# Even products ahead of the match-replaces, and the lag correlation through a stationary inverse matrix, a ScalarE copy and TensorE transposes

## What is computed

```
corr = ifft(fft(q) * conj(fft(k))).real        # q = layernorm(x), k = v = ctx, along the 64 positions
w, idx = top_k(corr, 8); w = softmax(w)        # per sequence and channel, 8 of 64 lags
out = sum_i w[i] * v[min(idx[i] + pos, 63)]    # the context shifted by each chosen lag
x = x + out
x = x + moe(layernorm(x))                      # 2 of 16 experts a token, and a shared expert
```

## Time and profile before

| | us |
|---|---|
| median of 3 runs | 483.29 (482.85 to 485.19) |
| profiled execution | 485.63 |
| its span | 483.7 |

### The profile page before, as it was taken

The page is one execution under the profiler, slowest core; times in us unless marked ns, Lnnn a source line. Parts: engine busy times, 40 slices in busy tenths (PEclk is TensorE's granted clock), DMA queues, the critical chain, the costliest instruction groups (busy, mean ns, idle before and its releaser), DMA issues.

```text
span 483.7 us, 9087 instructions
## 1 busy us (share of the span) xinstructions
PE 434.3 (90%) x2640; PEld 335.3 (69%) x2640; DVE 303.2 (63%) x960; ACT 217.5 (45%) x456; POOL 256.4 (53%) x311
## 2 busy tenths in 40 slices
PE   4698888888888887899999989999999899999992
PEld 2445555555555555478888969998889899878891
DVE  3768888888888877468676234443343443426975
ACT  4545666556666563263022114464454565722120
POOL 2556666666666663002787500778857561044772
PEclk9889999999999999999999998999999999999997
DMA  8411244444444432061776654788888885255896
GB/s 325 175 45 65 68 152 154 152 168 171 173 171 172 169 126 74 22 252 76 246 274 231 226 197 117 251 268 291 303 286 294 244 272 177 100 158 169 271 300 211
DMA packets 39295, 91.83 MB, mean 190 GB/s; under 512 B 4432, under 2 KB 4432, under 8 KB 39120
## 3 DMA queue, kind: packets, MB, share of 16 engines
q1 hardware_dynamic: 32256, 64.25, 37.7%
q0 software_dynamic: 6992, 27.01, 17.8%
HBM read 49.82 MB, written 41.42 MB: 189 GB/s over the span
## 4 chain that ended last, share of the span: by engine, by line
PE 58%; DVE 18%; DMA 10%; issue 5%; POOL 4%; ACT 3%; DVEq 0%; POOLq 0%; SPq 0%; ACTq 0%
PE bank L408 33%; DMA y_rows<-sh_act 7%; PE bank L427 7%; PE bank L444 6%; DVE arena L887 5%; DVE top_v L877 4%; PE bank L572 3%; PE bank L417 3%; PE bank L419 3%; DMA arena<-y_rows,pos_i 2%; DVE arena L883 2%; POOL arena L1235 2%; PE bank L493 2%; DVE arena L893 2%; DVE arena L892 2%
## 5 line engine op out<-in xcount | busy, mean ns | idle before, releaser
L408 PE MATMUL bank<-tokens_hi,shw_hi 128*128 128x512 f32 (+1 forms) x160 | 56.3, 352 | 0.0
L408 PE MATMUL bank<-tokens_hi,shw_lo 128*128 128x512 f32 (+1 forms) x160 | 55.6, 347 | 0.0
L408 PE MATMUL bank<-tokens_lo,shw_hi 128*128 128x512 f32 (+1 forms) x160 | 55.6, 347 | 0.0
L1235 POOL DMA_INDIRECT arena<-y_rows,pos_i x32 | 32.4, 1013 | 42.2 <-DMA y_rows<-sh_act 27.2
L408 PE MATMUL bank<-w_hi,tokens_hi 128*128 x188 | 53.9, 287 | 0.6 <-issue 0.5
L408 PE MATMUL bank<-w_hi,tokens_lo 128*128 x188 | 53.7, 285 | 0.0
L408 PE MATMUL bank<-w_lo,tokens_hi 128*128 x188 | 53.6, 285 | 0.0
L1212 POOL DMA_INDIRECT xs_rows<-x2T,pos_i x32 | 37.0, 1156 | 28.8 <-DVE pos_i L1003 19.3
L1051 DVE TENSOR_TENSOR act_sb<-bank,silu_sb 128x128 f32<-128x128 f32 x47 | 13.7, 292 | 56.7 <-ACT silu_sb L759 51.5
L1198 POOL TENSOR_TENSOR w_lo<-x2T,w_hi 128x1536 fp32r<-128x1536 f32 x13 | 45.5, 3499 | 1.1
L1038 DVE TENSOR_TENSOR tokens_lo<-bank,tokens_hi 128x512 fp32r<-128x512 f32 x47 | 32.5, 692 | 19.8 <-ACT tokens_hi L753 19.6
(11 more groups left out here) (138 smaller groups left out, 1101.7 us busy)
## 6 DMA issues: line engine op xcount, KB each, us to landing
y_rows<-sh_act SPq DMA_DIRECT2D x47, 256.0 KB, 4.0
xs_rows<-act_lo SPq DMA_DIRECT2D x10, 1024.0 KB, 4.8
x2T<-w_exp POOLq DMA_DIRECT2D x13, 768.0 KB, 5.8
xg_sb<-xs_rows SPq DMA_DIRECT2D x24, 256.0 KB, 3.3
const_sb<-xs_rows SPq DMA_DIRECT2D x23, 256.0 KB, 4.6
resid<-x SPq DMA_DIRECT2D x16, 256.0 KB, 2.7
arena<-ctx SPq DMA_DIRECT2D x16, 256.0 KB, 3.3
x_rows<-arena SPq DMA_DIRECT2D x16, 256.0 KB, 2.1
```

Of the source, the lines that this page charges most:

```text
L408: last = mm(ps, a[i], b[k], start=start and n == 0, stop=stop and n == len(terms) - 1)
L1235: nc.gpsimd.indirect_dma_start(y_in[buf], None, y_rows[:, :], bass.IndirectOffsetOnAxis(ap=pos_i[:, col:col + 1], axis=0)).then_inc(y_gath ...
```

## The change

In the correlation, `C["corr"]` becomes the stationary matrix and the 512 channels stream, in two products (one for each sequence) into the halves of `ps_T`. The result has lags in the partitions. ScalarE copies it to `corr_prod[0]` at the head of its iteration, and four TensorE transposes turn it into `ps_corr`, in the form it had. Two semaphores are added, and a wait for the last reader of `ps_T`. On VectorE the match-replaces of pair `n` go behind the even products of pair `n − 1`.

```diff
--- before.py
+++ after.py
@@ -264,6 +264,7 @@
         w_even_psum, w_odd_psum = sem("w_even_psum"), sem("w_odd_psum")
         out_products_ready, out_psum, resid_ready = sem("out_products_ready"), sem("out_psum"), sem("resid_ready")
         x2n_ready, x2T_psum, x2T_ready = sem("x2n_ready"), sem("x2T_psum"), sem("x2T_ready")
+        lags_psum, lags_ready = sem("lags_psum"), sem("lags_ready")
         logits_psum, logits_ready = sem("logits_psum"), sem("logits_ready")
         route_step, route_diff, route_exp = sem("route_step"), sem("route_diff"), sem("route_exp")
         chosen_ready, counts_psum = sem("chosen_ready"), sem("counts_psum")
@@ -439,10 +440,14 @@
                     p, _ = pair(h, b, 0)
                     pe.wait_ge(products_ready, p + 1)
                     wait(pe, lags_marked, p)
+                    wait(pe, x2T_ready, p - 2)
+                    for s in range(2):
+                        last = mm(ps_T[s * L:(s + 1) * L, :], C["corr"], corr_prod[s], start=True, stop=True)
+                    last.then_inc(lags_psum, 1)
+                    pe.wait_ge(lags_ready, p + 1)
                     for c in range(KB):
-                        for s in range(2):
-                            last = mm(ps_corr[:, c * P + s * L:c * P + (s + 1) * L], corr_prod[s][:, c * P:(c + 1) * P], C["corr"],
-                                      start=True, stop=True)
+                        cols = slice(c * P, (c + 1) * P)
+                        last = nc.tensor.transpose(ps_corr[:, cols], corr_prod[0][:, cols], C["identity"])
                     last.then_inc(corr_psum, 1)
                 if n == PAIRS:
                     shared_half(0, 0, 0, range(2, KB))
@@ -678,6 +683,10 @@
                     normalise(0, xn, tile_of(resid, p), p, xn_ready)
 
             def iteration(h, b, n):
+                if live(n, 0):
+                    p, _ = pair(h, b, 0)
+                    act.wait_ge(lags_psum, p + 1)
+                    copy(corr_prod[0], ps_T[:, :]).then_inc(lags_ready, 1)
                 if live(n, -1):
                     p, _ = pair(h, b, -1)
                     act.wait_ge(lagwT_psum, p + 1)
@@ -881,16 +890,19 @@
                     largest = tops[:, :, 0:1]
                     tt(segs(top_e[:, :]), tops, largest.to_broadcast([P, SEGS, TOPK]), ALU.subtract)
                     tt(segs(expz), lags, largest.to_broadcast([P, SEGS, L]), ALU.subtract).then_inc(centered, 1)
-                    wait(dve, lagwT_psum, p)
-                    apart(dve, dve_passed)
-                    for s in range(SEGS):
-                        last = nc.vector.match_replace(segs(lagw)[:, s], tops[:, s], lags[:, s], TAKEN)
-                    last.then_inc(lags_marked, 1)
                 if live(n, -1):
                     p, pb = pair(h, b, -1)
                     dve.wait_ge(w_even_psum, p + 1)
                     tt(out_prod[0], ps_w_even[0][:, :], ctx_even[pb][0], ALU.mult)
                     tt(out_prod[1], ps_w_even[1][:, :], ctx_even[pb][1], ALU.mult).then_inc(out_products_ready, 1)
+                if live(n, 0):
+                    p, _ = pair(h, b, 0)
+                    wait(dve, lagwT_psum, p)
+                    apart(dve, dve_passed)
+                    lags, tops = segs(ps_corr[:, :]), segs(top_v[:, :])
+                    for s in range(SEGS):
+                        last = nc.vector.match_replace(segs(lagw)[:, s], tops[:, s], lags[:, s], TAKEN)
+                    last.then_inc(lags_marked, 1)
                 if n == 0:
                     products(h, b, n)
                 if live(n, 0):
```

## The result

| | before | after |
|---|---|---|
| median (runs) | 484.24 us (4) | 508.1 us (4; 507.31 to 508.76) |
| ratio after to before | | 1.049, 95% interval 1.0447 to 1.0534 |
| profiled execution, its span | 485.63, 483.7 | 507.31, 505.5 |
| granted clock over the span | 0.984 | 0.946 |
| TensorE busy (share) | 434.3 (90%) | 443.1 (88%) |

The change costs 23.9 us. The forecast was 497.3 with a range of 491 to 503: the direction was right, and the time lies above the range. Of the 10.8 us between them, 1.0 is the median of before, 484.24 here and 483.29 in the forecast.

The account below looks back on a forecast made before the run. The prediction took the longest circle of dependences in a loop turn to bound the kernel. Start +5.7, twelve turns +9.6 and end −1.3 made +14.0 us on 483.3, so 497.3 us, range 491 to 503.

Parts of the forecast that it names:

- The circle through ScalarE: Maxima, VectorE's list, GpSimd's root, normalisation, copy, transposes, maxima: 12.31 us a turn against 11.51, +9.6 us over 12 turns.
- The signs named for it: Copy 0.72 us behind normalisation, TensorE idle near 1.8 before transposes, VectorE some 1.5 before maxima, turn 12.3 us.
- rival C: Clock falls in the loop: about 1.9 us a turn, 520 us if every turn, 503 if three; chance 0.06.
- Rival B: Copy partly held, no wait before L892, start at full clock: 11.9 us a turn, 490.9 us; chance 0.10.
- The new wait before the even products: On VectorE, L892 waits 0.28 us for the even lag spectrum, which the match-replaces hid; bounds 0 and 0.45.
- The later marks: VectorE's marks come later by two even products; costed at nothing, up to 1.2 us without cover.
- Rival A: Copy not held, TensorE's circle decides: about 11.2 us a turn, 480.7 us in all; chance 0.08.
- The start: Up to the maxima of pair 2, at 40.6 instead of 34.86: +5.7 us, lower clock expected.
- The lower bound of 4.2 us: Least cost forecast up to the maxima of pair 2, reckoned with TensorE at full clock: +4.2 us.
- The end: Turn of pair 14: VectorE's 1.70 us wait before L917 shrinks, giving back 1.3 us (0.5 to 1.5).

Follow-up runs that it names:

- The order alone: Kernel before with only the match-replaces moved behind the even products, old correlation kept: 483.63 us beside 489.92, ratio 0.986.
- the correlation alone: Changed kernel with the match-replaces put back ahead of the even products, so only the new correlation: 500.73 us beside 489.92, ratio 1.0194.
- the filled kernel: Changed kernel plus eight TensorE products of constants between the correlation products and the wait for the copy: 504.59 us beside 489.92, ratio 1.0268.
- the second execution: Changed kernel run once more with nothing altered, beside the kernel before: 508.65 us beside 485.52, ratio 1.0486.
- the kernel with the copy first: Changed kernel with ScalarE's new copy moved ahead of the normalisation of x from pair 1 on: 486.09 us beside 489.92, ratio 0.9928.

## Why the prediction was right and wrong

*The circle through ScalarE: right.* Forecast 12.31 us a turn, measured 12.27 wherever the clock was full. The links held one by one: moments to normalisation 90.05 − 88.46 = 1.59 (forecast 1.58), normalisation to copy 0.72 (0.72), copy to transposes 91.38 − 90.77 = 0.61 (0.69), transposes to maxima 0.81 (0.77). The signs named for it are there in the turns at the full clock, with two differences of size: TensorE's idle time before the transposes was 2.0 and not 1.8, since the products came earlier than reckoned, and VectorE's before the maxima was 1.76 and not 1.5. The sign of rival C was there too: the clock from pair 2 to pair 14 was 0.89. Rival B, a circle only partly held with 11.9 us a turn, falls with the 12.27.

*The new wait before the even products: right.* Forecast 0.28 us; in the changed kernel L896 waits for the spectrum,

```profile
82.11 0.69 DVE L896 TENSOR_TENSOR arena<-bank,arena 128x512 f32<-128x512 f32 x1 [0.18 <-PE bank L428]
```

with 0.18 us idle and the rest of the 0.28 in handing over.

*The two halves apart: right.* The order alone gave 10.86 us a turn (10.7 in the expectation), the correlation alone 11.99 (12.0). The later marks, which the sum costs at nothing, were not tested apart.

*Rival A: rightly rejected; its price came out by luck.* With the copy unheld the kernel stood at 0.993 of before; the rival had said 480.7 us, which is 0.993 of 484.24. But its terms were off both ways: the twelve turns gave 131.35 − 138.07 = −6.7 us where it had −3.6, and the turn of pair 14 took 14.26 us instead of 12.78, +1.5 where it had −1.3.

*The start: right in size.* Maxima of pair 2 at 39.90 (40.6 forecast), with the lower clock as expected there. The lower bound of 4.2 us was ill worked out: by the rows that the forecast uses, the full clock takes off 1.1 us before the even spectrum and 0.94 before L892, which leaves 3.7.

*The end: wrong.* Forecast −1.3 us, measured +0.6. The clock explains part of it; but with the clock at 1.00 the turn still took 12.55 us, −0.2, in the filled kernel and in the second execution of the changed one. In the filled kernel the two subtractions (L931, L917 of before) started early, as forecast, and were slower:

```profile
197.57 2.51 DVE L931 TENSOR_TENSOR tokens_lo<-x2T,tokens_hi 128x512 fp32r<-128x512 f32 x2 [0.52 <-ACT tokens_hi L739]
197.93 1.60 POOL L1161 TENSOR_TENSOR tokens_lo<-x2T,tokens_hi 128x512 fp32r<-128x512 f32 x1
```

They took 2.51 us where they had taken 1.77, beside GpSimd's subtraction, which took 1.60. Already before, the two engines had met, but for less time: GpSimd's subtraction ended 0.62 us behind the start of L917. Clear of each other the two subtractions take 1.29 us, as in the kernel with the copy first, where GpSimd had finished at 178.78:

```profile
181.56 1.27 POOL L1147 TENSOR_TENSOR tokens_lo<-x2T,tokens_hi 128x512 fp32r<-128x512 f32 x1
...
179.49 1.29 DVE L934 TENSOR_TENSOR tokens_lo<-x2T,tokens_hi 128x512 fp32r<-128x512 f32 x2 [2.84 <-ACT tokens_hi L742]
```

(The first row is of the kernel before, the second of the one with the copy first.) The earlier start of VectorE's work made the meeting 0.74 us dearer; another 0.4 is idle time that stayed before the subtractions (0.52 us of the 1.70), and in the first execution the clock took 0.8 more.

*The clock: the step that failed.* The sum had no term for it. It stood as rival C with a chance of 0.06, and it came, in eight of twelve turns, for 9.3 us; with it the sum is 497.3 + 9.3 = 506.6, against 508.1 measured. The filled kernel is the forecast without it: 1.0268 × 484.24 = 497.2 us, with an interval of 494.8 to 499.6. The price in C, 1.9 us for a turn, holds for the dearest turns (14.17 − 12.27 = 1.90); the eight cost 1.2 us each in the mean, since the lower clock covers only a part of a turn. What was wrong was the weight. I saw that TensorE would stand 1.85 us in one piece, and set against it a single stretch at the loop's end that had kept the clock. TensorE's pause in that stretch was 1.80 us; in the kernel with the order alone the pause at the same place was 2.45, and there the clock fell (0.80 from 182 to 190 us):

```profile
189.30 0.66 PE L493 MATMUL bank<-const_sb,arena 128*128 128x128 f32 x4 [1.80 <-ACT arena L659]
...
181.42 0.75 PE L493 MATMUL bank<-const_sb,arena 128*128 128x128 f32 x4 [2.45 <-ACT arena L659]
```

A single case that goes well is no evidence for a gap that comes back twelve times. And I compared busy shares, which the correlation alone shows to be a poor guide here: the same 9.85 us of work in a turn kept the clock with its idle time in two pieces.

The Trainium skill (TensorE: Matmul & The Clock Gate, HAM oscillation) describes a case of this kind: idle gaps between bursts bring half rate back, burst after burst. Its gaps are waits for data, longer than the 2.0 us here, so the prediction read the section wider than it stands when it had C come in every turn. The runs agree in kind (the clock fell again and again with the gap of 2.0 us, never in the steady turns of the kernels with gaps of up to 1.3). In degree they don't: it was low in eight turns of twelve in either profiled execution, not in each turn, so the 520 us are about as far off as my 497.

Why not in each turn, the table shows: a turn that has lost the clock mostly leaves a shorter pause for the next one. This limits the cost by itself, and neither the sum nor C had it. Not settled: why a fall costs 2.1 us in one turn and 0.6 in another behind the same pause of 2.0, and why the second execution lost the clock at pair 2 behind a pause of 1.58. No run changed the length of the pause with everything else the same, so that its length decides is a reading of the table.

## What to carry to other kernels

Before adding an instruction to an engine with idle time, look at what stands directly ahead of it in that engine's order and what that one waits for: here ScalarE was idle for 1.84 us, and the copy still came late, because the idle time was a wait of the instruction ahead. A gap that a change opens on TensorE in every turn of a loop belongs into the sum with the lower clock's price, not among the unlikely rivals. And take the halves of a change apart: one was worth 1.4%, and the whole lost 4.9%.

## What was not expected of the hardware

That more work makes the kernel faster: 2.05 us of useless products in each turn, on the engine that is busiest, saved 9 to 11 us of 508.

That VectorE's subtractions wait for GpSimd's. The two subtractions of the tokens took 1.29 us clear of GpSimd's subtraction, 1.77 in the kernel before and 2.51 beside L1161, by how long the two ran together; the small L882 took 0.23 us before, and 0.69 in the kernel with the order alone, where GpSimd's L1176 ran at the same time (89.74 to 91.01):

```profile
89.74 1.27 POOL L1176 TENSOR_TENSOR act_lo<-arena,act_lo 128x512 fp32r<-128x512 f32 x1
```

L882 ended at 91.08, just behind GpSimd's instruction; in the kernel with the copy first it started 0.34 us before the end of the same GpSimd instruction and took 0.43. So it looks as if it stood until GpSimd was through. In return GpSimd's L1161 took 1.60 us where it took 1.26 clear of them. L883, which starts right behind, kept its 0.68, and beside GpSimd's instructions on one element a partition (L1124, 0.55 us) L882 kept its 0.23. Both slowed instructions read two operands from SBUF, and L883 one from PSUM. The Trainium skill (GPSIMD Engine Reference, Specifications) says that GpSimd's SBUF interfaces are shared with VectorE and contended by instructions with two SBUF inputs; the rows agree. A forecast that moves such an instruction in time has to ask what GpSimd does then.
